# Depth of the activation loads and packing of the parameter vectors in a two-layer recurrent network kernel

## What is computed

```python
xn = _layernorm(x)
s = _L0_attn_ref(xn, ...)        # token shift, second layernorm, k and v of width 64, a scan over tokens
g = _silu(_L0_ffn_ref(xn, W1, b1, W2, b2))   # ternary weights, 1024 -> 4096 -> 1024, gelu
x = x + s * g
xn = _layernorm(x)
s = _L1_attn_ref(xn, W_x, b_x, W_dt, b_dt, A_log)   # ternary weights, activations rounded to 8 bits, cumulative product and sum
g = _silu(_L1_ffn_ref(xn, weight))                  # ternary weight
x = x + s * g
```

## Time and profile before

| | |
|---|---|
| median of 2 runs | 2292.13 us (2290.82 to 2293.44) |
| the profiled execution | 2299.64 us |
| its span on the slowest core, core 5 | 2298.1 us |
| spans of the 8 cores | 2288.0 to 2298.1 us |
| busy: DVE, PE, ACT | 1365.7 us (59%), 978.7 us (43%), 707.4 us (31%) |
| HBM read, written | 135.25 MB, 16.78 MB |
| longest parts of the chain that ended last | DVE 34%, PE 30%, ACT 11%, DMA 10% |

### The profile page before, as it was taken

The page is one execution under the profiler, slowest core; times in us unless marked ns, Lnnn a source line. Parts: engine busy times, 40 slices in busy tenths (PEclk is TensorE's granted clock), DMA queues, the critical chain, the costliest instruction groups (busy, mean ns, idle before and its releaser), DMA issues.

```text
span 2298.1 us, 17873 instructions; the slowest of 8 cores (2288.0 to 2298.1 us)
## 1 busy us (share of the span) xinstructions
PE 978.7 (43%) x3686; PEld 365.5 (16%) x3686; DVE 1365.7 (59%) x1722; ACT 707.4 (31%) x949; POOL 26.2 (1%) x52
## 2 busy tenths in 40 slices
PE   0321132213999999995103114125145054153250
PEld 0000000101333333331000003011012021021020
DVE  1124467663444444445622773776977878878877
ACT  0543321006556556532275000002132132131220
POOL 0000000000000000000100000000000000000000
PEclk9999999756999999997557555557577577576675
DMA  2876800003232333323740000000011011010000
GB/s 33 244 205 186 231 4 0 0 0 113 94 106 95 108 106 98 100 83 89 166 140 20 0 0 0 28 1 25 21 37 46 17 48 41 14 55 37 0 37 37
DMA packets 70290, 153.20 MB, mean 67 GB/s; under 512 B 18771, under 2 KB 27092, under 8 KB 68117
## 3 DMA queue, kind: packets, MB, share of 16 engines
q1 hardware_dynamic: 65318, 126.89, 19.1%
q0 software_dynamic: 4864, 25.17, 3.4%
HBM read 135.25 MB, written 16.78 MB: 66 GB/s over the span
## 4 chain that ended last, share of the span: by engine, by line
DVE 34%; PE 30%; ACT 11%; DMA 10%; issue 8%; DVEq 4%; ACTq 1%; SPq 0%; PEldq 0%; PEld 0%; POOL 0%; POOLq 0%
PE psB L784 10%; PE psA L767 8%; PE psA L1038 5%; DVE poolf L374 5%; DMA poolf<-w2t 4%; DVEq L110 3%; PE psA L1019 3%; ACT poolb L584 2%; ACT poolf L556 2%; ACT poolb L512 2%; DVE poolf L673 2%; ACT poolf L559 2%; PE psB L1119 2%; ACT poolb L776 2%; DMA poolf<-xT 2%
## 5 line engine op out<-in xcount | busy, mean ns | idle before, releaser
L784 PE MATMUL psB<-poolb 128*128 128x512 bf16 x1024 | 254.8, 379 | 42.9 <-ACTq L110 32.8
L797 DVE TENSOR_TENSOR poolb<-psB,poolb 128x512 bf16<-128x512 f32 x224 | 154.8, 691 | 182.8 <-PE psB L784 182.2
L1119 PE MATMUL psB<-poolb 128*128 128x512 bf16 x256 | 70.5, 438 | 431.1 <-ACTq L110 431.1
L556 ACT ACTIVATE poolf<-poolf 128x512 f32<-128x512 f32 (+1 forms) x160 | 143.9, 899 | 353.9 <-DVEq L110 285.1
L767 PE MATMUL psA<-poolb 128*128 128x512 bf16 x1024 | 231.5, 384 | 12.5 <-DVEq L110 12.5
L562 DVE TENSOR_SCALAR poolb<-poolf 128x512 bf16<-128x512 f32 (+1 forms) x160 | 76.8, 480 | 141.3 <-ACTq L110 127.3
L623 PE MATMUL psC<-poolf 1*128 1x512 f32 x32 | 29.7, 1026 | 296.1 <-DVEq L110 244.7
L512 ACT ACTIVATE poolb<-poolf 128x1024 bf16<-128x1024 f32 x96 | 101.5, 1057 | 125.2 <-DMA poolf<-w2t 59.4
L559 ACT ACTIVATE poolf<-poolf 128x512 f32<-128x512 f32 (+1 forms) x160 | 129.2, 807 | 25.9 <-ACTq L110 25.9
L1126 ACT ACTIVATE poolf<-psB,poolf 128x512 f32<-128x512 f32 x32 | 22.0, 688 | 354.3 <-DVEq L110 321.7
L767 PEld LDWEIGHTS psA<-poolb 128*128 128x128 bf16 x1024 | 100.8, 99 | 137.7 <-issue 19.5
(11 more groups left out here) (188 smaller groups left out, 1515.4 us busy)
## 6 DMA issues: line engine op xcount, KB each, us to landing
poolf<-w2t SPq DMA_DIRECT2D x64, 512.0 KB, 3.3
poolf<-xT SPq DMA_DIRECT2D x96, 256.0 KB, 4.8
poolf<-w1t SPq DMA_DIRECT2D x32, 512.0 KB
poolf<-w1t SPq DMA_DIRECT2D x64, 256.0 KB, 3.2
poolf<-wxt SPq DMA_DIRECT2D x16, 512.0 KB, 5.1
poolf<-wdtt SPq DMA_DIRECT2D x16, 512.0 KB, 4.8
poolf<-wft SPq DMA_DIRECT2D x16, 512.0 KB, 4.7
x1spill<-poolf POOLq DMA_DIRECT2D x32, 256.0 KB, 4.9
```

Of the source, the lines that this page charges most:

```text
L556: aop(lambda e: e.activation(sa.ap(0, ncols), stg.ap(off, off + ncols), Act.Relu, scale=rv.ap(), bias=Mb_v.ap()), [wk, rv.key(), Mb_v.key( ...
L784: pop_(lambda e, c=c, j=j, pbk=pbk, w2q8=w2q8, h8=h8: e.matmul(psB_t[:, pbk:pbk + 512], w2q8.ap(j * 1024 + c * 128, j * 1024 + (c + 1) * 128),
L797: vop(lambda e, pbk=pbk, oa=oa: e.tensor_add(oa.ap(), psB_t[:, pbk:pbk + 512], oa.ap()), [kB(pbk, pbk + 512), oa.key()], [oa.key()])
L1119: pop_(lambda e, c=c, g=g, dc2=dc2, pbk=pbk: e.matmul(psB_t[:, pbk:pbk + 512], wfq.ap(dc2 * 1024 + c * 128, dc2 * 1024 + (c + 1) * 128), x ...
```

## The change

The eight vectors are packed on the host into one array `vpack` of 128 x 74 float32. One load brings it into `tbuf`, and eight DVE copies bring its columns to where the vectors were loaded to before. The copies stand ahead of the chain L404 to L445 on DVE.

The pieces of `xT` of both passes go through all four places of `wstage`, place `i % 4`. `xnext()`, called for the piece i, first issues every load up to piece i + 3 that hasn't been issued, then hands out piece i. The list `_xpl` has the pieces of both passes, so the loads run on from one pass into the other.

```diff
+    vpk = I("vpack", [128, 74])
...
-        load_pp(tsg_r, v_tsg)
-        load_pp(lnw_v, v_lnw)
...
-        load_pp(tfv, v_tf, p=64)
+        dma_in(tbuf.ap(0, 74), vpk, tbuf.key(0, 74))
+        vp_off = 0
+        for reg, w in ((tsg_r, DC), (lnw_v, DC), (lnb_v, DC), (alog_r, DC),
+                       (b2_v, DC), (b1_v, 32), (tdv, 1), (tfv, 1)):
+            vop(lambda e, reg=reg, o=vp_off, w=w: e.tensor_copy(reg.ap(), tbuf.ap(o, o + w)),
+                [tbuf.key(vp_off, vp_off + w)], [reg.key()])
+            vp_off += w
...
+        _xpl = [(c, g) for g in range(G) for c in range(DC)] * 2
+        _xis = [0]
+
+        def x_prefetch(upto):
+            while _xis[0] < min(upto, len(_xpl)):
+                i = _xis[0]
+                c, g = _xpl[i]
+                xpiece(c, g, i % 4)
+                _xis[0] += 1
+
+        def xnext():
+            i = pi[0]
+            x_prefetch(i + 4)
+            stg = wstage.sub((i % 4) * 512, GW)
+            pi[0] += 1
+            return stg
 
         def ln1_src(c, g, par):
-            stg = xpiece(c, g, pi[0] % 2)
-            pi[0] += 1
+            stg = xnext()
...
             for c in range(DC):
                 pump(1)
-                stg = xpiece(c, g, pi[0] % 2)
-                pi[0] += 1
+                stg = xnext()
```

More of the change, by code:

```diff
@@ L1189, in _host_layout @@
         v_alog=np.asarray(inputs["L1_attn_A_log"], f32),
+        vpack=np.concatenate(
+            [np.asarray(inputs[k], f32).reshape(-1, 128).T for k in
+             ("L0_attn_time_shift_gates", "L0_attn_ln_w", "L0_attn_ln_b",
+              "L1_attn_A_log", "L0_ffn_b2", "L0_ffn_b1")] +
+            [np.pad(np.asarray(inputs[k], f32).reshape(-1, 64).T, ((0, 64), (0, 0)))
+             for k in ("L0_attn_time_decay", "L0_attn_time_first")], axis=1),
         c_ident=np.eye(128, dtype=f32),
```

## The result

| | before | changed |
|---|---|---|
| median of all runs | 2297.4 us (10 runs) | 2348.3 us (11 runs) |
| ratio | | 1.023 (95% interval 1.0197 to 1.0264) |
| profiled execution, its span | 2299.6, 2298.1 us | 2347.8, 2346.3 us |
| statistics pass, a step, mean of the 8 cores | 3.38 us | 4.15 us |
| apply pass, a step, mean of the 8 cores | 3.20 us | 3.98 us |

What follows compares the result with a forecast made beforehand. Computing nearly sets the statistics pass, w pieces the apply pass. Held w adds 17.7 and 20.6 us, ends +2 and -2, packed load -1.3: +37 us, 2329 us median; own range 2314 to 2340, whole range 2292 to 2352.

Steps and rivals of the forecast that it cites:

- second rival: Both passes: w transfers get no shorter, L stays 5.3 us, steps 4.11 and 4.21, together 2345 us; chance 0.2.
- The hold: Both passes: w issued behind x, 2.78 us (statistics) and 2.97 us (apply) after the abs began, 1.47 and 1.67 later.
- The landing time L: Both passes: a w piece's time from issue to landing, taken as 4.8 us; steps of 3.86 and 3.96 us.
- The ends: Ends of the prefetch: w1 lands later at the start, +2 us; last three w free of the wait, -2 us.
- The sum: Whole kernel: 17.7 + 20.6 + 2 - 2 - 1.3 = +37 us; 2336.6 us profiled, 2329 us median.
- The rival of the hidden hold: Both passes: L falls to 3.3 us, so the later w issue hides; -3.4 us per pass, 2286 us; chance 0.15.
- The rival of unshortened transfers: Both passes: L stays 5.3 us, statistics +25.7 us, apply +28.6 us, together 2345 us; chance 0.2.
- The rival of the ring of four semaphores: Both passes: x(i+3) also waits for x(i+1) to land, holding w later; +5 us, 2334 us; chance 0.05.
- The start: Program head: packed load lands at 4.8 us, copies take 2 us, first scaled kwt at 16.2 instead of 17.55; -1.3 us.
- The waits for x: Apply pass: DVE's 8.8 us of waits for x go, already counted inside the step differences.

## Why the prediction was right, and where its sizes were off

- **How near it came.** +37 us was forecast and 51 to 53 measured. The measured median of 2348.3 us lies in the whole range (2292 to 2352) with 4 us to spare, but outside the forecast's own, 2314 to 2340: it stands where the second rival had put it, and is in the whole range only because that rival was taken into it. At 1.023 the change is on the far side of 2%, to which the prediction gave 0.25. So the mechanism was foreseen and the size was not. Of the 19 us between 2329 and 2348.3, 5 are the median before, 2292.1 on two runs and 2297.4 on ten.
- **The hold.** Right, to 0.01 us: w 2.78 and 2.97 us after the abs began were worked out, 2.77 and 2.97 stand in the trace, and the issue gap of 0.48 with them. SP's waits moved from ACT to DVE.
- **The landing time L.** This is the term that was mis-sized, in "I take 4.8". The landings in the traces average 5.25 us in the statistics pass and 5.1 in the apply pass, (5.25 + 0.14 + 2.78) / 2 = 4.09 and (5.1 + 0.14 + 2.97) / 2 = 4.11 a step, where 3.86 and 3.96 were forecast. The reasoning behind 4.8 was that longer steps leave the DMA engines idler and w lands sooner. They are idler, 72% and 67% busy, and w doesn't land sooner than before (4.9 and 5.1). It does when x's bytes don't go right ahead of it: 3.5 to 3.6 without them, 4.2 to 4.4 with them behind. The x pieces, now ahead, land sooner in its place (median 4.2 us, where the earlier trace rows had 4.9).
- **The ends.** The table's 4.15 and 3.98 us hide that both passes run at the same pace. Without the first step the statistics pass has 4.07 us a step; without the last three, whose w are free of the wait, the apply pass has 4.09. The first step, from cast to cast, went from 3.1 to 6.4 us, because w1 now leaves behind x3: +3.3, where +2 was forecast.
- **The sum.** On the mean of the cores the last multiply comes 48 us later. The first step gives 3.3 of it, the 30 others of the statistics pass 30 x (4.07 - 3.39) = 20, the apply pass 31 x (3.98 - 3.20) = 24. Forecast for the same were 2, 17.7 and 20.6 - 2. Part of the apply pass's shortfall is the base: 3.32 was core 5's, the mean of the cores was 3.20. The 786 KB per step of the prediction are 768 KB in its own unit, which nothing in the sum uses.
- **The cores.** In the two profiled executions the spans of the cores lie 10 us apart before and 23 after. In the other executions on record they lie 8 to 28 us apart before (34 executions) and 16 to 39 after, so little can be built on it.
- **The rival of the hidden hold** (L at 3.3, 2286 us) fell: L would have had to be under 3.6, and is near that only without x's bytes. The Trainium skill (DMA: Bandwidth & Descriptors, Anatomy of one DMA) fits one DMA, issued from GpSimd, by 2.0 us and its bytes at 436 GB/s: 3.2 us for w alone. An estimate by the same formula for the bytes of w and x together is 3.8. The first is near the 3.6 of that run; the second is far from the 5.1 to 5.25 measured, so the formula doesn't carry over to two loads back to back on SP's queue with eight cores loading.
- **The rival of unshortened transfers** (L 5.3, 2345 us) is what came: 5.3 was its L and 5.25 and 5.1 were measured. It had 0.2. Its argument, w behind an x in every case, was the right one.
- **The rival of the ring of four semaphores** left 12 waits of SP for xT, 9.7 us in all, in the whole stretch, under 0.2 us a step. With two pieces ahead, where w isn't held, 19 such waits, 15.2 us, cost nothing that the total shows.
- **The start.** Forecast -1.3 us; measured -0.14 between the two profiled cores, -0.5 on the mean of the cores. The packed load was to land at 4.8 and its copies began at 6.61. That is 3.7 us from issue, so it isn't like a kwt piece, which lands in 1.7. The copies were forecast at 2 us and took 2.3 with the gap behind them, the chain 7.5 and took 7.5 (8.94 to 16.39), and what follows it 1.9 and took 1.0. Why the load takes 3.7 us was not tried; v_tsg, issued at the same time before, was waited for until 6.38.
- **The waits for x** went, all 8.8 us of them, and nothing was gained by it, as forecast. The runs with two ahead and with w ahead show how much they were worth: 0.1 us a step in the apply pass.

What stays open: how x's bytes delay w. The runs show that they do, and that L is shorter where x left 2.9 us before w than where it left 0.5 to 2.2 us before, but not by which part of the path.

## What to carry to other kernels

A queue that issues in order hands every wait on to what stands behind it. Before a load is moved ahead, ask which event frees its place, and whether that comes later than the event that frees the place of the next load in the queue: with p places and a depth of d, piece i+d waits for the reader of i+d-p, so d = p - 1 waits for the step just past, d = p - 2 for the one before. Deepen the stream that is late (w, by the chain of waits), and put its load ahead of the one that is early.

## What the runs showed of the hardware

- A 512 KB load 0.48 us behind a 256 KB load on one queue, all eight cores loading, took 5.1 to 5.25 us from issue to landing on average; 4.2 to 4.4 when the last 256 KB load had left 2.9 us before; and 3.5 to 3.6 behind a load of 8 KB (128 x 16 float32).
- The DMA engines' busy share didn't tell which of the first two it was: in the statistics pass L was 5.25 us at 72%, 4.9 at 85% and 4.4 at 82%. Only in the run without x's bytes was the share low too (55%, 164 GB/s).
- The same passes moved 241 to 248 GB/s on a core at 88 to 91% when four buffers kept the queue full, so 237 GB/s at 85% in the kernel before was not the limit. Each w then took longer to land (5.7 us on average), but on that core ACT waited for w1t only 4 times from 35 to 140 us, 4.9 us in all.
- The first load of 296 bytes for each of 128 partitions took 3.7 us from issue to its reader at the program's start, where loads of 256 bytes for each took 1.6 to 1.8 us to land later on.
